# Routing of the second layer's tokens placed between the last steps of the attention before it

## The chip, the core and the metric

The kernel runs on one core of a Trainium2 chip. The metric is the device time in microseconds (us) of one execution, measured from outside the core; smaller is better. The engines are PE (TensorE, matrix products and transposes), ACT (ScalarE), DVE (VectorE), POOL (GpSimd) and SP (SyncE, which here only issues DMA transfers). Each has its own stream of instructions and takes them in order; they wait for one another by semaphores.

## What is computed

The reference is a stack of two layers over 2048 tokens of 256 values, each layer an attention on a small context and then a feed-forward part with experts:

```python
x = x + tanh(g_xattn[0]) * L0_xattn(layernorm(x), ctx)
x = x + tanh(g_ffn[0])   * L0_ffn(layernorm(x))
x = x + tanh(g_xattn[1]) * L1_xattn(layernorm(x), ctx)
x = x + tanh(g_ffn[1])   * L1_ffn(layernorm(x))
```

`L1_ffn` takes the softmax of 16 router logits `x @ router_w.T` for each token, keeps the four best experts, and adds to their weighted outputs a shared network that is scaled by a sigmoid of one more logit. So the second routing needs, for every token, the mean and deviation of the x that the second attention has just updated.

## The kernel before, in words

The 2048 tokens are 16 tiles of 128, `NT = 16`, held in `x_sb`; a pair is two neighbouring tiles (pair 7 is tiles 14 and 15).

**The second attention** (`attn1_pe`, `attn1_act`, `attn1_dve`, `attn1_pool`, `attn1_sp`) goes over `NQ = 128` steps, 8 per tile, each with two of the 16 heads. In a step PE makes two banks of logits (L1291), DVE takes their minima (L1397), ACT the exponentials (L1364), SP issues one DMA transpose of them (L1534), and four steps later PE multiplies the transposed counts with the values (`weighted`, L1303, eight small products). Once a tile's eight steps are through, DVE normalises it (`normalised`, L1403 and L1405). Once a pair's two tiles are normalised, its **output chain** runs: four transposes on PE (`output_transposes`, L1312), a high half on ACT (`output_high`, L1370), the low half on DVE (`output_low`, L1412), two projections on PE (`project`, six products each of L269 and one for the bias, L275), the addition to x on DVE (`update`, L1418), and then mean and variance of the two tiles (`stats`, L252 and L255). The chains of the first seven pairs lie among the steps of later tiles. That of pair 7 has nothing left to lie among: the loops run 16 steps more, to `STEPS = NQ + 2 * PAIRS`, for it alone. At the end DVE adds epsilon to all 16 variances (`stats_end`, L259), and the engines meet at a barrier (`meet`).

**The second routing** starts there. POOL raises 16 columns to the power -0.5 (`inverse_deviation(4)`, L1797), DVE makes 16 biases from them (L437), and then `route_pe`, `route_act` and `route_dve` go over the eight pairs in order. A pair takes these steps, by which names the prediction calls them:

- *even*, ACT L421, and *odd*, DVE L440: the two tiles of the pair normalised into `xnf`;
- *turn*, PE L377: four transposes of 128x128 f32 into a bank of PSUM;
- *high*, ACT L425, and *low*, DVE L448: the transposed pair as two f16 halves in `xnT`;
- *logits*, PE L269 with `sb_rw`: twelve products of 17 columns;
- *scores*, DVE L452: the logits copied to `lg`.

SP writes each normalised pair to the token table in DRAM (`table_dma`, L634). After the last scores, PE begins the shared network's gate and up products (L269 with `sb_sgu`) and DVE the choice of the best experts (L462 and on). The first layer's routing runs through the same three functions.

Storage ties the routing to the attention. `xnf` holds the steps' counts and their transposes (tiles 0 to 7), and two sets of transposed queries (tiles 12 to 15). `xnT`, seen as f32 under the name `xn32`, holds the queries on their way, the normalised outputs `o_n` and the halves `o_hl` of the output chain.

## Time and profile before

| | |
|---|---|
| median of 3 runs | 922.58 us (921.42 to 922.62) |
| profiled execution, time | 927.97 us |
| profiled execution, span from first to last instruction | 926.2 us |
| PE busy | 730.8 us, 79% of the span |
| DVE busy | 689.0 us, 74% |
| POOL busy | 491.3 us, 53% |
| ACT busy | 440.2 us, 48% |
| mean granted clock of PE | 0.868 of full speed |

The profile comes from one execution, whose time is 5.39 us above the median. All start times are counted from its first instruction. A share of busy time says little here, since the stages are limited by different things; what the change touches lies between about 570 us (the last two tiles of the attention) and 631 us (the last scores). A chain of waits is a list, in order of time, of what the end of the program really hung on. A line can be that of a helper: L269 is every three-part product, so it is told apart by its operands.

### The profile page before, as it was taken

The numbers are of one execution on the slowest core, as the hardware profiler recorded it, in microseconds if no ns is written. First come the engines' busy times: TensorE is split into PE (matmuls) and PEld (weight loads), VectorE is DVE, ScalarE is ACT, GpSimd is POOL, SyncE is SP. The second block draws the span as 40 slices with busy tenths as digits, with TensorE's granted clock in tenths as the row PEclk, the third lists the DMA queues.
The fourth block names the chain that finished last, engine by engine and source line by source line (L and its number), as shares of the span: only waits on it lengthen the run. The fifth ranks groups of instructions, "written<-read, shape, count | busy, mean of one in ns | idle before, by whom it ended". The sixth has DMA issues, their size and how long they took to land.

```text
span 926.2 us, 18401 instructions
## 1 busy us (share of the span) xinstructions
PE 730.8 (79%) x5700; PEld 490.1 (53%) x5701; DVE 689.0 (74%) x1819; ACT 440.2 (48%) x1037; POOL 491.3 (53%) x607
## 2 busy tenths in 40 slices
PE   3469857678899799578787777658879999999992
PEld 1258745356665455234444444335657777775561
DVE  3968956756675866889989899838857777776774
ACT  3355324323332223588889899825133344442230
POOL 5285795556662756665444467010064444467772
PEclk9678975879999999688878897758979999999997
DMA  8024444823452221499999999921034444444334
GB/s 296 2 78 140 140 156 158 240 69 115 146 159 96 86 63 41 91 186 169 195 186 191 178 184 183 179 73 41 0 97 141 123 134 140 140 146 149 95 97 131
DMA packets 203258, 121.17 MB, mean 131 GB/s; under 512 B 146476, under 2 KB 194480, under 8 KB 203184
## 3 DMA queue, kind: packets, MB, share of 16 engines
q1 hardware_dynamic: 192816, 91.10, 40.5%
q0 software_dynamic: 10368, 29.14, 11.4%
q8 instruction: 38, 0.62, 0.3%
q14 instruction: 36, 0.29, 0.1%
HBM read 64.16 MB, written 32.98 MB: 105 GB/s over the span
## 4 chain that ended last, share of the span: by engine, by line
PE 28%; ACT 10%; DVE 8%; POOL 8%; issue 7%; DMA 4%; DVEq 2%; POOLq 1%; ACTq 0%; SPq 0%
PE PS L269 13%; POOL sb_region L720 7%; ACT sb_xnf L1364 4%; PE PS L815 4%; ACT sb_wkh L1364 3%; DVE sb_wk L1397 3%; PE PS L754 2%; DMA sb_xnf<-sb_xnf 2%; PE PS L778 2%; PE PS L1291 2%; PE PS L807 2%; PE PS L404 1%; DMA sb_wkh<-sb_wkh 1%; DVE sb_x_sb L905 1%; POOL sb_xnf L670 1%
## 5 line engine op out<-in xcount | busy, mean ns | idle before, releaser
L670 POOL DMA_INDIRECT sb_xnf<-token_table,sb_ids x120 | 115.8, 965 | 150.1 <-DVE sb_wk L970 64.8
L1397 DVE TENSOR_SCALAR_CACHE_REDUCE sb_wk<-PS 128x512 f16<-128x512 f32 x256 | 161.8, 684 | 8.2 <-PE PS L1291 6.2
L269 PE MATMUL PS<-sb_xnT,sb_sgu 128*128 128x512 f16 x528 | 126.8, 393 | 1.1 <-DVE sb_lg L452 0.6
L269 PE MATMUL PS<-sb_region,sb_wkh 128*128 x720 | 121.6, 320 | 5.3 <-issue 2.8
L838 ACT ACTIVATE sb_wk<-PS 128x512 f32<-128x512 f32 (+1 forms) x48 | 28.6, 596 | 141.6 <-PE PS L269 129.0
L269 PEld LDWEIGHTS PS<-sb_region,sb_wkh 128*128 128x128 f16 x720 | 69.3, 100 | 47.2 <-issue 14.3
L754 PE MATMUL PS<-sb_sdn,sb_wkh 128*128 128x256 f16 x544 | 72.4, 287 | 27.6 <-DVE sb_wkh L941 25.8
L1364 ACT ACTIVATE sb_wkh<-PS,sb_slotv 128x512 int16<-128x512 f32 x128 | 87.3, 705 | 12.2 <-DVE sb_wk L1397 9.5
L1364 ACT ACTIVATE sb_xnf<-PS,sb_slotv 128x512 int16<-128x512 f32 x128 | 86.9, 701 | 11.1 <-DVE sb_wk L1397 8.2
L269 PEld LDWEIGHTS PS<-sb_xnT,sb_sgu 128*128 128x128 f16 x528 | 52.5, 101 | 59.2 <-issue 8.4
L970 DVE SCALAR_TENSOR_TENSOR sb_wk<-PS,sb_sm,sb_wk 128x176 f32<-128x176 f32 x120 | 42.6, 396 | 53.5 <-ACT sb_wk L866 53.3
L754 PEld LDWEIGHTS PS<-sb_sdn,sb_wkh 128*128 128x128 f16 x544 | 54.9, 103 | 47.9 <-DVE sb_wkh L941 30.5
L815 PE MATMUL PS<-sb_region,sb_wkh 128*128 x600 | 76.3, 273 | 2.7 <-DVE sb_wa L983 2.2
L857 ACT ACTIVATE sb_wkh<-PS 128x512 f16<-128x512 f32 x60 | 35.8, 596 | 83.8 <-PE PS L778 83.8
L720 POOL DMA_INDIRECT sb_region<-slot_table,sb_place x64 | 65.4, 1022 | 18.9 <-issue 18.6
L866 ACT ACTIVATE sb_wk<-PS 128x352 f32<-128x352 f32 x60 | 27.8, 463 | 91.2 <-PE PS L269 91.2
L1291 PE MATMUL PS<-sb_wa,sb_xnf 128*128 128x512 f16 x88 | 39.7, 451 | 30.6 <-ACT sb_wkh L1364 18.7
L815 PEld LDWEIGHTS PS<-sb_region,sb_wkh 128*128 128x128 f16 x600 | 55.3, 97 | 14.8 <-issue 5.6
L933 DVE SCALAR_TENSOR_TENSOR sb_wk<-PS,sb_wk 128x512 f32<-128x512 f32 (+1 forms) x48 | 33.2, 692 | 39.9 <-ACT sb_wk L838 36.3
L1507 POOL TENSOR_TENSOR sb_region<-sb_stg,sb_region 128x704 f16<-128x704 f32 (+1 forms) x32 | 42.9, 1340 | 21.6 <-issue 18.5
L954 DVE TENSOR_TENSOR sb_wkh<-PS,sb_wkh 128x512 f16<-128x512 f32 x60 | 41.2, 687 | 17.1 <-ACT sb_wkh L857 16.5
L778 PE MATMUL PS<-sb_idf,sb_xnf 128*128 128x128 f32 x240 | 38.4, 284 | 17.6 <-DMA sb_xnf<-token_table,sb_ids 17.4
(290 smaller groups left out, 1638.6 us busy)
## 6 DMA issues: line engine op xcount, KB each, us to landing
slot_table<-sb_wa SPq DMA_DIRECT2D x60, 256.0 KB, 2.3
slot_table<-token_table SPq DMA_DIRECT2D x16, 640.0 KB
sb_stg<-gu SPq DMA_DIRECT2D x24, 352.0 KB, 4.2
sb_stg<-dn SPq DMA_DIRECT2D x24, 256.0 KB, 3.8
token_table<-sb_xnf SPq DMA_DIRECT2D x16, 256.0 KB, 4.9
sb_stg<-sgu SPq DMA_DIRECT2D x8, 352.0 KB, 5.4
sb_x_sb<-x SPq DMA_DIRECT2D x1, 2048.0 KB, 12.2
out<-sb_x_sb SPq DMA_DIRECT2D x16, 128.0 KB, 2.9
```

The costliest lines, as they stand in the source:

```text
L269: last = nc.tensor.matmul(out_, lhs(i, c), rhs(j, c), start=(c == 0 and n == 0 and not begun), stop=(c == C - 1 and n == 2 and not more))
L670: nc.gpsimd.indirect_dma_start(xg[l][:, 2 * (g % XR) + n, :], None, xw[l][:, :], bass.IndirectOffsetOnAxis(ap=ids[:, 2 * g + n:2 * g + n + ...
L720: nc.gpsimd.indirect_dma_start(y_pair[m][:, t % 2, :], None, ys[1][:, :], bass.IndirectOffsetOnAxis(ap=place[:, k, t:t + 1], axis=0))\
L754: last = nc.tensor.matmul(PS[:, first + i // 2, i % 2 * D:(i % 2 + 1) * D], wkh[:, HR * h + v, i * P:(i + 1) * P], sdn[:, j, k, :], start= ...
L778: last = nc.tensor.transpose(PS[:, 4 + s % 2, (2 * n + c) * P:(2 * n + c + 1) * P], xg[l][:, 2 * (s % XR) + n, c * P:(c + 1) * P], idf[:, :])
L815: last = nc.tensor.matmul(PS[:, 7, n * D:(n + 1) * D], wkh[0:r, 4 + 2 * u + i, (2 * c + n) * P:(2 * c + n + 1) * P], DN[l][0:r, bass.ds(e[ ...
L954: nc.vector.tensor_tensor(wkh[:, 2 * (s % 2) + 1, :], PS[:, 4 + s % 2, :], wkh[:, 2 * (s % 2), :], ALU.subtract).then_inc(e_xl[l].sem, 1)
L970: last = nc.vector.scalar_tensor_tensor(wk1[:, 2 + u, n * EI:(n + 1) * EI], PS[:, 2 * u + n, EI:EG], wv[u][:, n:n + 1], wk1[:, u, n * EI:( ...
L1291: nc.tensor.matmul(PS[:, (2 * s + h) % LB, :], q_iT[t % 3][:, pair, :], keys, start=True, stop=True).then_inc(h_qk, 1)
L1364: nc.scalar.activation(h_count[s % 4][:, h * CTX:(h + 1) * CTX], PS[:, (2 * s + h) % LB, :], ACT.Exp, scale=-1.0, bias=h_nb[u][:, h:h + 1] ...
L1397: nc.vector.tensor_scalar(h_any[(2 * s + h) % 6], PS[:, (2 * s + h) % LB, :], LEVELS, None, ALU.add, ALU.min, accum_out=h_nb[s % 3][:, h:h ...
L1507: nc.gpsimd.tensor_tensor(lo, w, hi, ALU.subtract).then_inc(stg_split[n % 4], 1)
```

## The change: what it does

The routing functions are cut into pieces (`route_turn`, `route_logits`, `route_even`, `route_high`, `route_scale`, `route_odd`, `route_low`, `route_scores`). For the first layer they are called in the same order as before. For the second layer, the calls are written out by hand behind the last attention step, among the steps of pair 7's output chain, and the barrier and the 16 extra steps of the loops are gone. The pairs come in the order 4, 5, 6, 0, 1, 2, 3, 7; in `route_turn` and the others `k` counts the places in that order, and the prediction's *turn(k)*, *low(k)* and so on go by it, so (7) is pair 7. Pairs 4, 5 and 6 are turned before the attention's last counts have left tiles 0 to 7 of `xnf`. The inverse deviations come in three pieces: 12 columns at step 113 of the attention on POOL, 2 columns behind its last step, and 2 behind the statistics of pair 7. To free `xnT`, `o_hl` gets a buffer of its own and the second `o_n` moves to `wk1`.

```diff
+        o_hl = sb("o_hl", [P, 2, 2 * D], F16)
...
+        PAIR_ORDER = (tuple(range(NT // 2)), (4, 5, 6, 0, 1, 2, 3, 7))
+        NM_ENDS = ((NT,), (NT - 4, NT - 2, NT))
+        NM_STEP = HEADS * (NT // 2 - 1) - 1
+
+        def scale_of(l, j):
+
+            return next(i + 1 for i, end in enumerate(NM_ENDS[l]) if 2 * j < end)
...
+        def route_turn(pe, l, k):
+            j = PAIR_ORDER[l][k]
+            at_least(pe, r_xn[l], 0, k + 1)
+            at_least(pe, r_xd[l], 0, k + 1)
+            at_least(pe, r_xl[l], 0, k - 1)
+            for c in range(C):
+                for i in range(2):
+                    last = nc.tensor.transpose(PS[:, k % 2, c * TB + i * P:c * TB + (i + 1) * P],
+                                               xnf[:, 2 * j + i, c * P:(c + 1) * P], idf[:, :])
+            last.then_inc(r_xT[l].sem, 1)
+
+        def route_logits(pe, l, k):
+            n = E[l] + 1
+            at_least(pe, r_xl[l], 0, k + 1)
+            at_least(pe, r_lgc[l], 0, k - 1)
+            for i in range(2):
+                t = 2 * PAIR_ORDER[l][k] + i
+                last = mm3(PS[:, 2 + k % 2, i * n:(i + 1) * n], lambda i, c: xnT[:, i, c, t * P:(t + 1) * P],
+                           lambda j, c: rw[l][:, j, c, :])
+            last.then_inc(r_lg[l].sem, 1)
...
+        def route_even(act, l, k):
+            t = 2 * PAIR_ORDER[l][k]
+            at_least(act, r_nm[l], 0, scale_of(l, t // 2))
+            nc.scalar.activation(xnf[:, t, :], x_sb[:, t, :], ACT.Identity, bias=nmr[:, t:t + 1],
+                                 scale=rstd[:, t:t + 1]).then_inc(r_xn[l].sem, 1)
...
-            act.wait_ge(rstd_ready, 2 + 3 * l)
-            at_least(act, r_nm[l], 0, 1)
...
+        def route_scale(dve, l, ready, first, end):
+            dve.wait_ge(rstd_ready, ready)
+            nc.vector.scalar_tensor_tensor(nmr[:, first:end], mv[:, first:end, 0], -1.0, rstd[:, first:end], ALU.mult, ALU.mult)\
+                .then_inc(r_nm[l].sem, 1)
...
-            for j in range(NT // 2):
-                at_least(sp, r_xn[l], 0, j + 1)
-                at_least(sp, r_xd[l], 0, j + 1)
+            for k, j in enumerate(PAIR_ORDER[l]):
+                at_least(sp, r_xn[l], 0, k + 1)
+                at_least(sp, r_xd[l], 0, k + 1)
...
-        o_n = [xn32[:, u * D:(u + 2) * D] for u in (2, 14)]
-        o_hl = xn32[:, 6 * D:8 * D].bitcast(F16).rearrange("p (h n) -> p h n", h=2)
+        o_n = [xn32[:, 2 * D:4 * D], wk1[:, 3, :]]
...
-            meet(pe, 3)
+            for k in range(BEHIND):
+                weighted(NQ - BEHIND + k)
+                if k < 3:
+                    route_turn(pe, 1, k)
+                if 1 <= k:
+                    route_logits(pe, 1, k - 1)
+            last_ = GROUPS - 1
+            output_transposes(last_)
+            route_turn(pe, 1, 3)
+            route_turn(pe, 1, 4)
+            project(last_, 0)
+            project(last_, 1)
+            route_logits(pe, 1, 3)
+            for k in range(5, NT // 2):
+                route_turn(pe, 1, k)
+                route_logits(pe, 1, k - 1)
+            route_logits(pe, 1, NT // 2 - 1)
...
-            meet(act, 3)
+            route_even(act, 1, 0)
+            route_even(act, 1, 1)
+            route_high(act, 1, 0)
+            route_even(act, 1, 2)
+            route_high(act, 1, 1)
+            at_least(act, h_pv, 0, NQ)
+            route_even(act, 1, 3)
+            route_high(act, 1, 2)
+            route_even(act, 1, 4)
+            output_high(GROUPS - 1)
+            route_high(act, 1, 3)
+            route_even(act, 1, 5)
+            route_high(act, 1, 4)
+            route_even(act, 1, 6)
+            route_high(act, 1, 5)
+            route_high(act, 1, 6)
+            route_even(act, 1, 7)
+            route_high(act, 1, 7)
...
+                if s == NM_STEP:
+                    stats_end(0, NM_ENDS[1][0])
+                if s == NM_STEP + 7:
+                    route_scale(dve, 1, 5, 0, NM_ENDS[1][0])
+            stats_end(NM_ENDS[1][0], NM_ENDS[1][1])
+            route_odd(dve, 1, 0)
+            route_odd(dve, 1, 1)
+            route_scale(dve, 1, 6, NM_ENDS[1][0], NM_ENDS[1][1])
+            route_low(dve, 1, 0)
+            route_odd(dve, 1, 2)
+            route_low(dve, 1, 1)
+            route_scores(dve, 1, 0)
+            normalised(NT - 1)
+            route_odd(dve, 1, 3)
+            route_low(dve, 1, 2)
+            route_scores(dve, 1, 1)
+            route_odd(dve, 1, 4)
+            output_low(GROUPS - 1)
+            route_low(dve, 1, 3)
+            route_odd(dve, 1, 5)
+            route_scores(dve, 1, 2)
+            route_low(dve, 1, 4)
+            route_odd(dve, 1, 6)
+            update(GROUPS - 1)
+            stats(NT - 2, NT - 1)
+            stats_end(NM_ENDS[1][1], NT)
+            route_scores(dve, 1, 3)
+            route_low(dve, 1, 5)
+            route_scores(dve, 1, 4)
+            route_low(dve, 1, 6)
+            route_scores(dve, 1, 5)
+            route_scale(dve, 1, 7, NM_ENDS[1][1], NT)
+            route_odd(dve, 1, 7)
+            route_scores(dve, 1, 6)
+            route_low(dve, 1, 7)
+            route_scores(dve, 1, 7)
...
+                if s == NM_STEP + 2:
+                    inverse_deviation(4, 0, NM_ENDS[1][0])
...
-            inverse_deviation(4)
+            inverse_deviation(5, NM_ENDS[1][0], NM_ENDS[1][1])
+            inverse_deviation(6, NM_ENDS[1][1], NT)
...
-            route_act(act, 1)
...
-            route_dve(dve, 1)
...
-            route_pe(pe, 1)
```

On PE, from the product of step 124 (L1303 before, L1337 after: `weighted`) to the shared network's first products (with `sb_sgu`). Before:

```order
L1303 MATMUL PS<-sb_Vi,sb_wkh 128x16 x16
L1303 MATMUL PS<-sb_Vi,sb_xnf 128x16 x16
L1312 MATMUL PS<-sb_idf,sb_xnT 128x128 x4
L269 MATMUL PS<-sb_wqp,sb_xnT 128x256 x6
L275 MATMUL PS<-sb_brow,sb_ones_h 128x256
L269 MATMUL PS<-sb_wqp,sb_xnT 128x256 x6
L275 MATMUL PS<-sb_brow,sb_ones_h 128x256
L377 MATMUL PS<-sb_idf,sb_xnf 128x128 x8
L269 MATMUL PS<-sb_rw,sb_xnT 128x17 x12
L377 MATMUL PS<-sb_idf,sb_xnf 128x128 x4
```

After, from behind the same product of step 124 (turns are L383, logits L270 with `sb_rw`, output transposes L1346):

```order
L383 MATMUL PS<-sb_idf,sb_xnf 128x128 x4
L1337 MATMUL PS<-sb_Vi,sb_wkh 128x16 x8
L383 MATMUL PS<-sb_idf,sb_xnf 128x128 x4
L270 MATMUL PS<-sb_rw,sb_xnT 128x17 x12
L1337 MATMUL PS<-sb_Vi,sb_xnf 128x16 x8
L383 MATMUL PS<-sb_idf,sb_xnf 128x128 x4
L270 MATMUL PS<-sb_rw,sb_xnT 128x17 x12
L1337 MATMUL PS<-sb_Vi,sb_xnf 128x16 x8
L270 MATMUL PS<-sb_rw,sb_xnT 128x17 x12
L1346 MATMUL PS<-sb_idf,sb_wk 128x128 x4
L383 MATMUL PS<-sb_idf,sb_xnf 128x128 x8
L270 MATMUL PS<-sb_wqp,sb_o_hl 128x256 x6
```

The products of steps 125 to 127 now stand behind turns and logits, and the output transposes behind the logits of three pairs; two more turns stand ahead of the projections.

On DVE, the end of the new order, from the update of pair 7 (L1484) to the choice of experts (L497); nmr is the bias column, lg the scores, and L463, L469, L476 are odd, low and scores:

```order
L1484 SCALAR_TENSOR_TENSOR sb_x_sb<-PS,sb_tgw,sb_x_sb 128x512
L253 BN_STATS sb_bst<-sb_x_sb 128x6 x2
L256 BN_AGGR sb_mv<-sb_bst 128x2 x2
L260 TENSOR_SCALAR sb_ve<-sb_mv 128x2
L476 TENSOR_SCALAR sb_lg<-PS 128x34
L469 TENSOR_TENSOR sb_xnT<-PS,sb_xnT 128x2x256
L476 TENSOR_SCALAR sb_lg<-PS 128x34
L469 TENSOR_TENSOR sb_xnT<-PS,sb_xnT 128x2x256
L476 TENSOR_SCALAR sb_lg<-PS 128x34
L458 SCALAR_TENSOR_TENSOR sb_nmr<-sb_mv,sb_rstd 128x2
L463 TENSOR_SCALAR sb_xnf<-sb_x_sb,sb_mv,sb_rstd 128x256
```

Behind the update only three scores and two lows stand between the epsilon (L260) and the bias of the last two tiles (L458); before, all eight pairs followed.

## Rows read from the trace of the kernel before

**Rows 1.** Chain of waits around the attention's last output chain: start us, us, what

```profile
601.29 3.09 DMA sb_xnf<-sb_xnf
...
604.43 0.40 PE PS L1303 x8
...
605.66 1.13 PE PS L1312 x4
...
606.81 0.61 ACT sb_xnT L1370
...
608.18 1.46 PE PS L269 x6
...
611.39 0.75 DVE sb_x_sb L1418
...
613.64 2.92 POOL sb_rstd L1797
```

**Rows 2.** Chain of waits through the second routing, same columns

```profile
616.95 0.61 ACT sb_xnf L421
617.65 1.10 PE PS L377 x4
618.77 0.61 ACT sb_xnT L425
619.40 0.70 DVE sb_xnT L448
620.15 0.49 PE PS L269 x12
...
630.21 0.51 PE PS L269 x12
```

**Rows 3.** Timeline of ACT: start, us, engine, line, operation [idle before <-releaser]

```profile
600.90 0.21 ACT L1364 ACTIVATION_READ_ACCUMULATOR sb_xnf<-PS,sb_slotv 128x1 f32 x1
...
616.95 1.09 ACT L421 ACTIVATE sb_xnf<-sb_x_sb,sb_nmr,sb_rstd 128x256 f32<-128x256 f32 x2 [9.54 <-DVE sb_nmr L437]
```

**Rows 4.** Timeline of DVE from the last maxima to the choice of experts

```profile
600.99 0.25 DVE L255 BATCH_NORM_AGGREGATE sb_mv<-sb_bst 128x2 f32<-128x6 f32 x2
...
616.75 0.73 DVE L440 TENSOR_SCALAR sb_xnf<-sb_x_sb,sb_mv,sb_rstd 128x256 f32<-128x256 f32 x2
...
622.27 0.69 DVE L448 TENSOR_TENSOR sb_xnT<-PS,sb_xnT 128x512 f16<-128x512 f32 x1 [0.78 <-ACT sb_xnT L425]
622.88 0.18 DVE L452 TENSOR_SCALAR sb_lg<-PS 128x34 f32<-128x34 f32 x1
622.98 0.40 DVE L440 TENSOR_SCALAR sb_xnf<-sb_x_sb,sb_mv,sb_rstd 128x256 f32<-128x256 f32 x1
...
630.74 0.19 DVE L452 TENSOR_SCALAR sb_lg<-PS 128x34 f32<-128x34 f32 x1 [0.49 <-PE PS L269]
```

**Rows 5.** Timeline of PE, same columns

```profile
601.86 0.38 PE L1303 MATMUL PS<-sb_Vi,sb_wkh 128*128 128x16 f16 x8 [1.03 <-DMA sb_wkh<-sb_wkh]
...
620.52 1.09 PE L377 MATMUL PS<-sb_idf,sb_xnf 128*128 128x128 f32 x4
621.40 0.52 PE L269 MATMUL PS<-sb_rw,sb_xnT 128*128 128x17 f16 x12
...
630.99 5.39 PE L269 MATMUL PS<-sb_xnT,sb_sgu 128*128 128x512 f16 x17 [0.29 <-DVE sb_lg L452]
```

**Rows 6.** POOL: groups by form (count, busy us, mean ns), and its timeline

```profile
L1797 POOL TENSOR_TENSOR sb_rstd<-sb_ve,sb_mhalf 128x12 f32<-128x12 f32 x1 | 2.3, 2307 | 6.5 <-DVE sb_ve L259 6.5
...
613.64 2.91 POOL L1797 TENSOR_TENSOR sb_rstd<-sb_ve,sb_mhalf 128x16 f32<-128x16 f32 x1 [30.39 <-DVE sb_ve L259]
```

**Rows 7.** Stretches: busy (count) of PE, PEld, DVE, ACT, POOL, then granted clock, DMA share

```profile
622.00:627.00 5.00, 4.68 (x51) 3.70 (x51) 3.84 (x10) 3.98 (x8) 0.00 (x0) 0.50 0.48 169
...
631.00:636.00 5.00, 5.00 (x17) 1.96 (x17) 4.76 (x51) 0.65 (x2) 0.00 (x0) 0.68 0.00 0
```

**Rows 8.** The page's DMA issues: KB each, median us to landing

```profile
token_table<-sb_xnf SPq DMA_DIRECT2D x16, 256.0 KB, 4.9
```

More of the change, by code:

```diff
@@ L413, in tiles_pe, with route_high @@
                              skip_group_check=True).then_inc(r_texp[l].sem, 1)
-        def route_act(act, l):
-            act.wait_ge(rstd_ready, 2 + 3 * l)
-            at_least(act, r_nm[l], 0, 1)
-            for j in range(NT // 2 + 1):
-                if j < NT // 2:
-                    t = 2 * j
-                    nc.scalar.activation(xnf[:, t, :], x_sb[:, t, :], ACT.Identity, bias=nmr[:, t:t + 1],
-                                         scale=rstd[:, t:t + 1]).then_inc(r_xn[l].sem, 1)
-                if j >= 1:
-                    at_least(act, r_xT[l], 0, j)
-                    nc.scalar.activation(xnT[:, 0, :, (j - 1) * TB:j * TB],
-                                         PS[:, (j - 1) % 2, :].rearrange("p (c n) -> p c n", c=C), ACT.Copy).then_inc(r_xh[l].sem, 1)
+        def route_even(act, l, k):
[3 more added lines that the diff above has]
+                                 scale=rstd[:, t:t + 1]).then_inc(r_xn[l].sem, 1)
+        def route_high(act, l, k):
+            j = PAIR_ORDER[l][k]
+            at_least(act, r_xT[l], 0, k + 1)
+            nc.scalar.activation(xnT[:, 0, :, j * TB:(j + 1) * TB],
+                                 PS[:, k % 2, :].rearrange("p (c n) -> p c n", c=C), ACT.Copy).then_inc(r_xh[l].sem, 1)
+        def route_act(act, l):
+            act.wait_ge(rstd_ready, 2)
+            for k in range(NT // 2 + 1):
+                if k < NT // 2:
+                    route_even(act, l, k)
+                if k >= 1:
+                    route_high(act, l, k - 1)
         def softmax_act(act, l):
@@ L456, in best_dve @@
+        def route_dve(dve, l):
+            route_scale(dve, l, 2, 0, NT)
+            route_odd(dve, l, 0)
+            for k in range(NT // 2 + 1):
+                if k + 1 < NT // 2:
+                    route_odd(dve, l, k + 1)
+                if k < NT // 2:
+                    route_low(dve, l, k)
+                if k >= 1:
+                    route_scores(dve, l, k - 1)
         def best_dve(dve, l):
@@ L1328, in attn1_pe @@
             at_least(pe, s_accr[0], 0, BLK)
-            for s in range(STEPS):
+            for s in range(NQ):
                 if s + AHEAD < NQ:
                     logits(s + AHEAD)
-                if BEHIND <= s < NQ + BEHIND:
+                if s >= BEHIND:
                     weighted(s - BEHIND)
@@ L1373, in attn1_act @@
             at_least(act, s_d[0], 0, NSH)
-            for s in range(STEPS):
+            for s in range(NQ):
                 t, pair = s // PAIRS, s % PAIRS
-                if s < NQ:
-                    exponentials(s)
+                exponentials(s)
                 if s == 1:
@@ L1418, in update @@
                 nc.vector.scalar_tensor_tensor(xt, o_bank, tgw[:, 1:2], xt, ALU.mult, ALU.add).then_inc(o_x, 1)
-            for s in range(STEPS):
+            for s in range(NQ):
                 t, pair = s // PAIRS, s % PAIRS
-                if s < NQ:
-                    maxima(s)
+                maxima(s)
                 if s < 2:
@@ L1454, in attn1_dve @@
                     stats(2 * o, 2 * o + 1)
-            stats_end(0, NT)
-            meet(dve, 3)
+                if s == NM_STEP:
[34 more added lines that the diff above has]
+            route_scores(dve, 1, 7)
         items = []
```

60 lines of the change are left out of this document (21 added, 39 removed).

## The prediction

> **What bounds the kernel now.** I read the chain of waits first, around the last attention step. The last transposed counts are issued at 601.29 and land for the product of step 127 at 604.43. Then comes a relay with one engine at work at a time: output transposes 605.66, high half 606.81, projections 608.18, update 611.39, statistics and epsilon, the power on POOL 613.64, the first even 616.95 [rows 1, 2]. The reader should see that each piece hands over to another engine, so that nearly every microsecond is latency. Then the second routing: even 616.95, turn 617.65, high 618.77, low 619.40, logits 620.15, eight pairs through the same ring, last logits 630.21, last scores 630.74 [rows 2, 4]. DVE's choice of experts and PE's shared products follow at once, the latter at 630.99 [rows 5]. From there DVE is busy 4.76 of 5 us [rows 7]. So the stretch from 601.29 to 630.74 lies bare on the path, and what follows should move with the last scores. The timelines of ACT, DVE and PE give the paces, the group of POOL the price of a power. The stretches give PE's clock: 0.50 of full speed through the routing [rows 7].
>
> **Step prices.** From start to start, in us, each from two rows. Even: 0.70 until PE can turn (616.95 to 617.65), about 0.5 until ACT takes the next (two last 1.09, one 0.61) [rows 2, 3]. Turn: 1.12 until ACT (617.65 to 618.77), 0.88 of PE (620.52 to 621.40) [rows 2, 5]. High: 0.63 until DVE (618.77 to 619.40), about 0.5 of ACT, taken as even's. Low: 0.75 until PE (619.40 to 620.15), 0.61 of DVE (622.27 to 622.88) [rows 2, 4]. Scores: 0.10 of DVE (622.88 to 622.98); odd: about 0.36 (two last 0.73) and, with the hand-over to PE, 0.45 until a turn [rows 4]. Logits: 0.53 until the scores (630.21 to 630.74) [rows 2, 4]; of PE I take 0.36, an estimate from their row of 0.52, whose last part overlaps what follows [rows 5]. The product of a step: 0.42 until DVE, 0.25 of PE, estimated the same way from 0.38 [rows 5]; normalising 0.81 until PE, so that product and normalising make the 1.23 from 604.43 to 605.66 [rows 1]. Output transposes 1.15 until ACT; high and low 1.37 together; the two projections 3.21 until the update (608.18 to 611.39), 1.47 of PE for the first; update, statistics and epsilon 2.25 until POOL (611.39 to 613.64), 2.0 of it on DVE [rows 1]. A check: the old loop, reckoned with these prices from 616.95, has its last scores at 630.60; they came at 630.74.
>
> **What the change costs and brings.** The removed parts are two. The 16-column power, the wait for it and the whole routing no longer follow the update; and two rounds of hand-over disappear with the barrier. Nothing is saved in work: all eight pairs are still turned. It is laid between the waits, in strict order on each engine, so I walk it through.
>
> *The start.* ACT's last exponential ends at 601.11 (600.90 + 0.21) [rows 3], and even(0), even(1) follow at 601.00 (the accumulator's read overlaps) and 601.50. DVE ends statistics of tiles 12 and 13 at 601.24 [rows 4], epsilon for two columns at 601.31, odd(0) at 601.40. Turn(0) starts at 601.85. POOL starts the two-column power at 601.57. Its price is not in the trace: 12 columns took 2.31, 16 took 2.92 [rows 1, 6], so a straight line gives some 0.8 for two, the top is 2.92. I take 1.2, nearer the low end, since the slope between the two rows is clear, with 0.4 for a fixed part. Then the bias comes at 602.8, ahead of low(0) at 603.60, and costs nothing. If the power took 2.9, low(0) and all behind it on DVE would wait.
>
> *The four last products.* They keep their inputs: step 125's came at 601.86, step 127's at 604.43 [rows 1, 5]. But on PE they now stand behind turns and logits: turn(0) 601.85, product 125 at 602.73, turn(1) 602.98, logits(0) 604.35 (waiting for low(0)), product 126, turn(2) 604.96, logits(1) 605.84, product 127 at 606.20. That is 1.8 later than before. DVE normalises at 606.62. Meanwhile high(2) waits on ACT behind the order that even(3) needs product 127: high(2) 607.12, low(2) 607.75, logits(2) 608.50, and only behind them the output transposes, at 608.86, 3.2 later than before. This is the price of the interleaving.
>
> *The output chain.* Turn(3) and turn(4) take PE until 611.52, which is when the projections start; the high and low halves (610.01 and 610.64, done at 611.38) are hidden behind them. Projections until 614.46, update at 614.70, 3.3 later than before. In those waits DVE and ACT have done the evens and odds up to (6) and the lows up to (4).
>
> *After the update.* DVE: statistics and epsilon until 616.78, then scores(3), low(5) 616.88, scores(4), low(6) 617.81, scores(5), bias 618.52. PE: logits(3), turn(5) 614.82, logits(4), turn(6) 616.06, logits(5) 617.63. POOL's last power starts at 616.95 and ends at 618.2, just inside DVE's own queue, so it costs nothing; at 2.9 it would end at 619.9. Then pair 7 alone: even 618.81, turn 619.51, high 620.63, low 621.26, logits 622.01, last scores 622.54.
>
> So update to last scores takes 7.8 instead of 19.3 (611.39 to 630.74), 11.5 gained, and 3.3 of that is given back by the later update. Sum: 630.74 - 622.54 = 8.2; the check above was 0.1 short, so I take **8.1**.
>
> *Beside other work.* The 12-column power at step 113 and its bias: POOL idles 30.39 before the old power [rows 6], so 2.3 plus its wait only push the last weight splits into that gap; if the gap were gone they would delay the shared weights, needed only at 622. DVE's share in the steps is two instructions of about 0.2, under 0.4 if none of it falls in a wait; against 8.1 I leave it in the range. SP's eight stores to the token table start at about 602 instead of 617; SP has the last transposes issued by then (601.29). They are needed at the row lists, 20 us after the last scores, and the last one now starts 1 us after even(7) as before. The new buffers move no work.
>
> Against the profiled execution the sum gives 927.97 - 8.1 = 919.9. That execution stands 5.4 above the median; nothing in the moved stretch explains those, so against the median it is 922.58 - 8.1 = **914.5**.
>
> **Rivals.**
> *PE's clock rises in the tail.* It was 0.50 in 622 to 627 although PE was busy 4.68 of 5; in 631 to 636, products without a break from 630.99, it averaged 0.68, so it went from 1.2 to 2.4 GHz after about 3.2 us [rows 7, 5]. In the walk PE has no gap from 608.86 to 616.9. If the clock rises at 613, PE's steps halve, but DVE's queue after the update holds: last scores 621.8, gain 8.9, 913.7; at the earliest, 612.5, they are at 621.05, 913.0. For it: the stretch is twice as long as 3.2. Against: five of its eight microseconds are turns and logits, during which the clock stayed down before.
> The Trainium skill's page "TensorE: Matmul & The Clock Gate" (section "Part 1: The HAM clock gate") says that the low rate is the default and that sustained activity releases it. By that rule this rival would come true; the stretch from 631 agrees, that from 622 does not.
>
> *The small powers cost as much as the large.* Two-column powers of 2.9 each: the bias at 604.6 holds low(0) by 1.0, and the second power adds 1.5 behind the scores. Walked through: last scores 625.05, gain 5.6, **917.1**. For it: 12 and 16 columns differ by only 0.6 [rows 1, 6]. Against: that is more than in proportion.
>
> *The stores collide with the last transposes (slower).* Three pairs' stores are issued before product 127, a store's median to landing is 4.9 [rows 8]. If the transposes of steps 125 to 127 each had to wait out one store, they would be 4.9, 9.8 and 14.7 late, and the walk ends at 635.5: 4.8 slower than before, **927.4**. It decides from 10 us of delay at product 127 on; less still leaves a gain, as PE comes to it 1.8 late anyway. Against: the transposes are issued first, on the same queue, and the stores moved at a DMA share of 0.48 [rows 7], far from full.
>
> *The gain is swallowed behind.* Some wait of the expert stage (stores, shared weights, first gathers) takes the 8 us back: 922.6. DVE's 4.76 of 5 [rows 7] speaks against.
>
> *The clock stays high from the start of the tail.* Everything on PE halves from 601.9 on: last scores 618.9, gain 11.7, 910.9. Nothing in the trace holds it up there.
>
> **Chances.** The walk 0.50, the clock's rise 0.22, the dear powers 0.15, clock high throughout 0.04, swallowed 0.06, collision 0.03. The range takes in the first three: from 913.0 less the spread of the runs shown (1.2) to 917.1 plus 1.2, **911.8 to 918.3**. A measurement can tell 0.2%, here 1.85 us, from no change. Faster by more: 0.50 + 0.22 + 0.15 + 0.04 = 0.91; within it 0.06; slower 0.03.
>
> **What would show it.** In the new profile: product 127 about 606.2 and update near 614.7, both later than before; the last scores near 622.5, with the steps behind unchanged in length; the two-column powers at 1.0 to 1.4; the last four products not waiting for DMA; a granted clock of 0.50 from 602 to 622. The forecast is wrong if the last scores keep their place, if a power of two columns takes 2 or more, or if the expert stage has a new wait.

## The result, and the profile after

| | before | changed |
|---|---|---|
| median | 922.60 us (921.42 to 925.54, 4 runs) | 913.02 us (912.74 to 915.69, 4 runs) |
| ratio | | 0.9892, 95% interval 0.9870 to 0.9915 |
| profiled execution: time, span | 927.97, 926.2 us | 915.69, 913.9 us |

The changed kernel is faster by 9.6 us, where 8.1 was forecast. The two profiled executions differ by 12.3, and 2.85 of this lies ahead of the change: the aggregate of tiles 12 and 13, the last thing both kernels do alike, starts at 600.99 before [rows 4] and at 598.14 now. The executions of one kernel spread by more than that ahead of this mark (e8 below), so I don't count it as the change's. I measure the **tail**, from the start of this aggregate to the start of the last scores, and subtract 2.85 from each time of the prediction's walk (its step-by-step times) before I compare. Before, the tail is 29.75 us.

The page of the changed kernel: the header, part 1, and the counts that say that no work went.

```profile
span 913.9 us, 18405 instructions
PE 729.3 (80%) x5700; PEld 490.9 (54%) x5701; DVE 692.0 (76%) x1823; ACT 440.6 (48%) x1037; POOL 494.2 (54%) x609
```

PE and DVE are as busy as ever. The time went out of the waits, and the chain of waits shows where (start us, us, what), against [rows 1, 2]:

```profile
599.10 1.10 PE PS L383 x4
...
602.09 0.21 PE PS L1337 x8
602.30 0.95 PE PS L383 x4
603.25 0.31 PE PS L270 x12
603.56 0.23 PE PS L1337 x8
...
606.16 0.95 PE PS L1346 x4
607.11 1.71 PE PS L383 x8
608.82 1.28 PE PS L270 x6
...
611.53 0.75 DVE sb_x_sb L1484
...
615.28 0.61 ACT sb_xnf L433
615.93 0.67 PE PS L383 x4
616.62 0.61 ACT sb_xnT L439
617.25 0.70 DVE sb_xnT L469
...
618.00 0.50 PE PS L270 x12
...
618.53 0.19 DVE sb_lg L476
```

In this stretch no DMA and no POOL stands in the chain any more. The first turn is where the chain had waited for a DMA transposition, product 127 (603.56, L1337) follows straight behind other work of PE, and behind the update there is one pair's ring, from 615.28 to 618.53, where there were eight. The timelines give the pieces that the prediction had timed. PE, with its longest wait ahead of the projections (for low(2)):

```profile
599.98 0.41 PE L1337 MATMUL PS<-sb_Vi,sb_wkh 128*128 128x16 f16 x8
603.41 0.36 PE L1337 MATMUL PS<-sb_Vi,sb_xnf 128*128 128x16 f16 x8
605.67 0.49 PE L270 MATMUL PS<-sb_rw,sb_xnT 128*128 128x17 f16 x12 [1.90 <-DVE sb_xnT L469]
606.01 1.09 PE L1346 MATMUL PS<-sb_idf,sb_wk 128*128 128x128 f32 x4
```

POOL, both small powers; and DVE from the aggregate to the last scores:

```profile
598.72 0.81 POOL L1898 TENSOR_TENSOR sb_rstd<-sb_ve,sb_mhalf 128x2 f32<-128x2 f32 x1 [15.53 <-DVE sb_ve L260]
613.77 0.70 POOL L1898 TENSOR_TENSOR sb_rstd<-sb_ve,sb_mhalf 128x2 f32<-128x2 f32 x1 [14.24 <-DVE sb_ve L260]
```

```profile
598.14 0.25 DVE L256 BATCH_NORM_AGGREGATE sb_mv<-sb_bst 128x2 f32<-128x6 f32 x2
...
599.56 0.16 DVE L458 SCALAR_TENSOR_TENSOR sb_nmr<-sb_mv,sb_rstd 128x2 f32<-128x2 f32 x1 [0.28 <-POOL sb_rstd L1898]
...
611.53 0.75 DVE L1484 SCALAR_TENSOR_TENSOR sb_x_sb<-PS,sb_tgw,sb_x_sb 128x512 f32<-128x512 f32 x1 [0.87 <-PE PS L276]
...
614.99 0.18 DVE L476 TENSOR_SCALAR sb_lg<-PS 128x34 f32<-128x34 f32 x1
615.09 0.15 DVE L458 SCALAR_TENSOR_TENSOR sb_nmr<-sb_mv,sb_rstd 128x2 f32<-128x2 f32 x1
...
618.53 0.19 DVE L476 TENSOR_SCALAR sb_lg<-PS 128x34 f32<-128x34 f32 x1 [0.58 <-PE PS L270]
```

The power was finished at 614.47, and the bias (L458) was taken at 615.09 without an idle time before it: DVE's own queue held it, as predicted. Last, stretches of the tail: busy us (count) of PE, PEld, DVE, ACT, POOL, then granted clock, DMA share, GB/s.

```profile
606.00:611.00 5.00, 5.00 (x31) 4.21 (x28) 2.76 (x7) 2.65 (x5) 0.00 (x0) 0.50 0.35 121
611.00:613.00 2.00, 2.00 (x36) 1.76 (x34) 1.38 (x3) 0.60 (x1) 0.00 (x0) 0.99 0.55 197
613.00:615.00 2.00, 0.51 (x13) 0.37 (x12) 1.85 (x9) 0.60 (x1) 0.70 (x1) 1.00 0.01 4
615.00:617.00 2.00, 0.94 (x16) 0.83 (x16) 0.66 (x5) 0.97 (x2) 0.00 (x0) 1.00 0.09 33
617.00:619.00 2.00, 0.71 (x13) 0.53 (x14) 1.18 (x6) 1.50 (x2) 0.00 (x0) 0.72 0.32 107
```

The clock went up at about 611.0, from 1.2 to 2.4 GHz, after five microseconds in which PE was never idle, and stayed up until after 617. So the prediction's first rival came true here, and not its base case of 0.50. The tail is 20.39 us, 9.36 shorter. From the last scores to the end of the span it is 295.4 us (913.9 - 618.53) against 295.5 before (926.2 - 630.74), so these two profiles show nothing given back. Second profiles of the same two kernels have 297.2 (e1) and 295.1 (e8), so this part alone is known to some 2 us only.

### The profile page after: what moved, and what is told of

Read it like the earlier page. It is cut to its first block, busy times and chain, and to the rows that moved or that the text cites. A ratio compares the mean times of both kernels' runs of the same rounds, so it can differ in the third digit from the quotient of the medians.

```text
span 913.9 us, 18405 instructions
## 1 busy us (share of the span) xinstructions
PE 729.3 (80%) x5700; PEld 490.9 (54%) x5701; DVE 692.0 (76%) x1823; ACT 440.6 (48%) x1037; POOL 494.2 (54%) x609
## 4 chain that ended last, share of the span: by engine, by line
PE 28%; DVE 9%; ACT 8%; POOL 8%; issue 7%; DMA 4%; DVEq 2%; POOLq 1%; ACTq 0%
PE PS L270 14%; POOL sb_region L755 7%; PE PS L850 4%; ACT sb_xnf L1414 4%; DVE sb_wk L1463 3%; ACT sb_wkh L1414 3%; PE PS L789 2%; DMA sb_xnf<-sb_xnf 2%; PE PS L813 2%; PE PS L1325 2%; DMA sb_wkh<-sb_wkh 2%; PE PS L842 2%; PE PS L419 1%; DVE sb_x_sb L940 1%; POOL sb_xnf L705 1%
## 5 line engine op out<-in xcount | busy, mean ns | idle before, releaser
L270 PE MATMUL PS<-sb_xnT,sb_sgu 128*128 128x512 f16 x528 | 128.1, 395 | 1.1 <-DVE sb_lg L476 0.6
L270 PE MATMUL PS<-sb_region,sb_wkh 128*128 x720 | 121.3, 320 | 5.1 <-issue 2.6
L270 PEld LDWEIGHTS PS<-sb_region,sb_wkh 128*128 128x128 f16 x720 | 69.2, 99 | 46.0 <-issue 13.1
L270 PEld LDWEIGHTS PS<-sb_xnT,sb_sgu 128*128 128x128 f16 x528 | 52.7, 101 | 59.8 <-issue 9.5
L989 DVE TENSOR_TENSOR sb_wkh<-PS,sb_wkh 128x512 f16<-128x512 f32 x60 | 41.2, 687 | 16.3 <-ACT sb_wkh L892 15.8
## 6 DMA issues: line engine op xcount, KB each, us to landing
sb_x_sb<-x SPq DMA_DIRECT2D x1, 2048.0 KB, 12.2
```

Of the source, the lines that this page charges most:

```text
L270: last = nc.tensor.matmul(out_, lhs(i, c), rhs(j, c), start=(c == 0 and n == 0 and not begun), stop=(c == C - 1 and n == 2 and not more))
L989: nc.vector.tensor_tensor(wkh[:, 2 * (s % 2) + 1, :], PS[:, 4 + s % 2, :], wkh[:, 2 * (s % 2), :], ALU.subtract).then_inc(e_xl[l].sem, 1)
```

## The experiments

**The theory** is the walk of the prediction, refined by the trace: the gain is latency taken out of two relays, about a third of it from cutting the power and the rest from laying routing into the waits, and some 3 us are lost again because the hand-written order lets PE wait for low(2) ahead of the output transposes. **Rivals**: most of the gain comes from the higher clock; the small powers matter more (or less) than thought; the stores, which now start earlier, hold up the last transposes.

All tails, from the aggregate of tiles 12 and 13 to the last scores, each from one profile; *product 127* and *update* are counted from the aggregate:

| kernel | aggregate at | product 127 | update | tail |
|---|---|---|---|---|
| before | 600.99 | 3.44 | 10.40 | 29.75 |
| e8 before, again | 591.95 | 3.53 | 10.49 | 29.84 |
| changed | 598.14 | 5.27 | 13.39 | 20.39 |
| e1 changed, again | 595.93 | 5.27 | 13.18 | 20.18 |
| e6 changed, stores held | 593.68 | 5.27 | 13.48 | 20.48 |
| e2 pieces only | 595.99 | 3.45 | 10.47 | 26.52 |
| e3 dear powers | 599.39 | 6.91 | 14.08 | 23.81 |
| e4 reordered | 597.50 | 5.12 | 11.32 | 17.75 |
| e5 reordered, stores held | 595.99 | 5.15 | 11.37 | 17.79 |
| e7 reordered, clock kept | 597.62 | 5.20 | 10.88 | 17.76 |
| e9 reordered, DVE +24 | 597.70 | 5.05 | 11.25 | 17.68 |
| e10 reordered, ACT +24 | 595.04 | 3.40 | 9.61 | 16.04 |
| e11 as e5, again | 596.36 | 5.00 | 11.21 | 17.63 |

**e8** is the kernel before, once more.

> The kernel before once more, for its profile alone. In its first profile the aggregate of tiles 12 and 13 starts at 600.99, in the four profiles of changed kernels at 595.9 to 599.4. If that is the spread of executions, this one starts between 596 and 601 and the stretch from there to the last scores is 29.7 us again. If the change also speeds up the steps before, it is at 600 or above.

918.64 us (span 916.9), one execution. Its tail is 29.84, within 0.1 of the other profile's, but it starts at 591.95, below the 596 to 601 that were expected, where the other one started at 600.99. So the way to the tail differs by up to 9 us between executions of one kernel, and the tail doesn't: a comparison of whole times says little about a change of 2 us, one of tails says it well. **e1** is the changed kernel once more.

> The changed kernel again, on the chip of the next three runs, so that they can be compared with it and not only with the kernel before. Both theories: 0.989 of the kernel before, within 0.9870 to 0.9915. On the clock: if its rise at the end of the projections belongs to the order of the work, it stands again between the first projection and the update, and last statistics of step 127 to last scores takes 20.1 us within 0.8; if it was luck, the clock stays at 0.50 and the stretch takes 21.3.

915.60 us, ratio 0.9899 (0.9871 to 0.9926). Tail 20.18, again with the clock's rise.

**e2** keeps the power in three pieces and the new buffers, but puts the routing behind the statistics again, in the new order of pairs:

```diff
-            for k in range(BEHIND):
-                weighted(NQ - BEHIND + k)
-                if k < 3:
-                    route_turn(pe, 1, k)
-                if 1 <= k:
-                    route_logits(pe, 1, k - 1)
+            weighted(NQ - BEHIND + 0)
...
+            weighted(NQ - BEHIND + 3)
             output_transposes(last_)
...
+            route_turn(pe, 1, 0)
...
```

> All routing steps stand behind pair 7's update (in the order 4, 5, 6, 0, 1, 2, 3, 7); the inverse deviations stay in three pieces and the barrier stays away. Theory of the walk: product 127 and the projections come back to their old places (no delay of 3.3 us), the power and its wait (3.3 us from 613.38 to the first even) leave the path, and the whole routing loop follows: 3.3 us faster than the kernel before, 5 to 6.5 slower than the changed kernel. Rival, that most of the gain is the power in pieces and the barrier's going: at least 7 us faster than before, within 2.5 of the changed kernel.

920.53 us, ratio 0.995 (0.992 to 0.998). The tail is 26.52, 3.23 shorter than before, where 3.3 was expected; and product 127 and the update keep their distance from the aggregate. So of the 9.36 of the change, 3.2 belong to the pieces, the barrier and the new order of pairs together, and 6.1 to the interleaving, net of what it gives back; the rise of the clock, which e2 doesn't have (0.50 from 599 to 623), is part of these 6.1. By medians e2 is only 4.9 slower than e1, just under the 5 to 6.5 that were expected; whole times spread too much to decide between 4.9 and 6.1.

**e3** puts a 16-column power of spare numbers, which nobody reads, ahead of each two-column power.

```diff
+                if n >= 5:
+                    nc.gpsimd.tensor_tensor(spare[:, n - 5, :], lower[:, 0, 0:NT], mhalf[:, :], ALU.pow)
                 nc.gpsimd.tensor_tensor(rstd[:, first:end], ve
```

> A power of 16 columns into a spare buffer ahead of each of the two-column powers (2.9 us more each; nothing of the result hangs on it). Theory of the walk: the first holds low(0) by 2.0 us, the second the last even by about 2.5; together 3.5 to 4.0 us slower than the changed kernel. Rival, that the powers are hidden well enough for their size not to matter: slower by less than 1 us.

919.22 us, ratio 0.9932 (0.9910 to 0.9954). Its timelines of POOL and of DVE:

```profile
599.96 3.02 POOL L1900 TENSOR_TENSOR sb_spare<-sb_lower,sb_mhalf 128x16 f32<-128x16 f32 x1 [15.65 <-DVE sb_ve L261]
602.95 0.70 POOL L1901 TENSOR_TENSOR sb_rstd<-sb_ve,sb_mhalf 128x2 f32<-128x2 f32 x1
```

```profile
603.68 0.16 DVE L459 SCALAR_TENSOR_TENSOR sb_nmr<-sb_mv,sb_rstd 128x2 f32<-128x2 f32 x1 [3.15 <-POOL sb_rstd L1901]
...
619.29 0.16 DVE L459 SCALAR_TENSOR_TENSOR sb_nmr<-sb_mv,sb_rstd 128x2 f32<-128x2 f32 x1 [2.19 <-POOL sb_rstd L1901]
```

The tail is 3.4 longer than the changed kernel's, a little under the 3.5 to 4.0 that were expected (3.6 by the medians of e3 and e1). About 0.5 of this isn't the power's own: from bias to last scores e3 takes 3.91 where the change takes 3.44, because the clock is at 0.50 from 618.5 on. Against the change the idle time before the bias is 3.15 instead of 0.28, and 2.19 instead of none. So the price of the power decides as the prediction's second rival said, and only where it exceeds what DVE has queued; at 0.70 to 0.81 it is free.

**e4** leaves the work as it is and changes the order alone: the output transposes, and all that they wait for, stand ahead of low(2).

```diff
-PE:  w0 turn0 w1 turn1 logits0 w2 turn2 logits1 w3 logits2 out turn3 turn4 p0 p1 logits3 turn5 logits4 ...
+PE:  w0 w1 turn0 turn1 w2 w3 turn2 logits0 out turn3 turn4 p0 p1 logits1 turn5 logits2 turn6 logits3 logits4 ...
-DVE: odd0 odd1 scale low0 odd2 low1 scores0 norm odd3 low2 scores1 odd4 outlow low3 ...
+DVE: odd0 odd1 scale odd2 low0 norm odd3 low1 odd4 low2 outlow scores0 low3 low4 ...
```

(These two pairs of lines sum up the calls, and are not the kernel's text. w0 to w3 are products 124 to 127, out the output transposes, p0 and p1 the projections. ACT's order is changed to match.)

> The same steps in another order, found by laying the same step prices out again: on PE turns (0) and (1) behind the product of step 125, product 127 directly behind 126, and the output transposes behind only one set of logits; the scores gathered behind the update. Theory of the walk: product 127 is at its old place (1.8 us earlier than in the changed kernel), the update 2.9 us earlier, last scores 3.5 us earlier: 3.5 us (3.0 to 4.0) faster than the changed kernel, 0.985 of the kernel before. Rival, that what bounds the tail is DVE's own work behind the update and not the place of the update: within 1 us of the changed kernel.

912.52 us, ratio 0.9867 (0.9840 to 0.9893). The tail is 2.6 shorter than the changed kernel's, where 3.5 was expected. The chain has the missing part:

```profile
597.80 4.77 DMA sb_xnf<-sb_xnf
...
602.62 0.38 PE PS L1337 x8
```

The transposed counts of step 127 took 4.77 us from issue to landing, where they had taken 3.09 before [rows 1]. In the changed kernel this is covered, since product 127 comes late anyway. I took it for the collision that the prediction's third rival had named, at a third of its price, and tried it.

**e5** and **e6** hold back every store to the token table until ACT, DVE and PE have done with step 127's product; e5 in the order of e4, e6 in the change's.

```diff
+            if l == 1:
+                at_least(sp, h_pv, 0, NQ)
             for k, j in enumerate(PAIR_ORDER[l]):
```

> The reordered kernel with SP holding the eight stores to the token table until the product of step 127 is done. In the reordered kernel without this, the transposition of step 127 took 4.77 us from its issue instead of 3.09 and PE waited 1.8 us for it, with DMA engines full. Theory, that the stores take DMA time from the last transposes: product 127 comes 3.4 us after the start of the last two-tile aggregate (604.43 - 600.99 before), the last transposition takes 3.1 to 3.3 us, and the stretch from that aggregate to the last scores is 17.0 us or a little less instead of 17.75, with the update 1 to 1.7 us earlier. Rival, that the late transposition was chance or comes from what ACT and PE do: it takes 4.8 again and nothing moves.

> The changed kernel with the same hold on SP. There product 127 stands behind 1.8 us of routing on PE, so a transposition that is 1.7 us late is just hidden. Theory: no difference from the changed kernel, stretch from the aggregate of tiles 12 and 13 to the last scores 20.2 to 20.4 us; the stores' later end is needed by nobody. Rival, that the stores cost the changed kernel as well: 1 us or more shorter.

e5: 908.86 us, ratio 0.9852 (0.9832 to 0.9871); e6: 913.10 us, ratio 0.9904 (0.9885 to 0.9924). In e5 the transposition is as late as ever, with no store anywhere near it:

```profile
596.34 4.76 DMA sb_xnf<-sb_xnf
...
601.14 0.38 PE PS L1339 x8
```

The tail is 17.79, that of e4. So it isn't the stores that make the transposition late, and my explanation fell. e6's tail is 20.48, that of the changed kernel to 0.1. That e5's median is 3.7 below e4's is no merit of the wait: the tails are equal, and e11, the same kernel in another job, had 912.05.

**e7** is meant to hold PE's clock up: three products of 512 columns, which nobody reads, are added to each of the steps 120 to 127 and to two of the last four products, in the order of e5.

```diff
+            def warm():
+                for n in range(3):
+                    nc.tensor.matmul(PS[:, 7, :], idh[:, :], wqp[:, 0, 0, :], start=True, stop=True)
...
+                if s >= NQ - 8:
+                    warm()
```

> The kernel with the reordering and the hold, and in addition three products of 512 columns that nobody reads behind each of the steps 120 to 127 of the loop and behind two of the last products, so that PE's clock is not let down. Theory: the granted clock stays at 1.0 from the last steps to the projections, turns take 0.44 us of PE instead of 0.88, projections 0.8 instead of 1.5, and the stretch from the aggregate to the last scores is 15.5 to 16.5 us. Rival, that DVE and ACT set the tail and PE's rate does not matter there, or that the products cost what they bring: 17 us as without them.

910.82 us, ratio 0.9868 (0.9848 to 0.9887). Two of its stretches, columns as above:

```profile
596.00:599.00 3.00, 2.69 (x35) 1.42 (x34) 2.52 (x11) 2.72 (x8) 0.80 (x1) 1.00 1.02 191
602.00:605.00 3.00, 1.79 (x28) 1.45 (x28) 1.71 (x5) 1.79 (x4) 0.00 (x0) 1.00 0.29 98
```

The tail is 17.76, against 17.79 in e5, where the clock was 0.50 for the first ten microseconds. But e7 didn't hold the clock to the end, as a later stretch and the same part of e5 show:

```profile
612.40:615.40 3.00, 2.01 (x28) 1.43 (x28) 1.68 (x5) 2.24 (x3) 0.00 (x0) 0.50 0.28 93
```

```profile
611.00:612.60 1.60, 1.04 (x20) 0.72 (x17) 1.10 (x4) 1.32 (x4) 0.00 (x0) 1.00 0.36 124
```

And pair 7's turn, in the chain of e7 and in that of e5:

```profile
612.34 1.11 PE PS L383 x4
```

```profile
611.19 0.66 PE PS L383 x4
```

Counted from the aggregate, e7 is 0.48 ahead of e5 at the update and still at the bias (13.87 against 14.35). It loses 0.45 of it in pair 7's ring, which takes 3.89 from bias to last scores at the low rate, and 3.44 in e5 at the high one. So the equal tails are two effects of the clock that cancel: 0.5 ahead of the update and 0.45 behind it. The rival "it is all the clock" is not borne out for the reordered kernels, since each effect is small against the 12 us by which e5's tail is shorter than that of the kernel before. But PE's rate does matter there, and with the clock up to the end the tail should be 0.45 shorter (an estimate from these two rings; no run shows it). For the change's own order it wasn't tried; there the trace gives the clock's share (below).

**e9, e10, e11** go after the late transposition. In the records of completions, 15 of its 16 parts land in time (in e5 by 599.53) and one at 601.10; before, all 16 land together. In each of the seven profiles so far with routing mixed in, a packet of 16 KB of instructions starts 0.42 to 0.50 us ahead of the 15th part; in the three others it starts over a microsecond behind the landing. So I tried to move that packet, on the guess that DVE's or ACT's stream fetches it: 24 instructions more, which write a tile that nobody reads, on DVE (e9) or ACT (e10), some hundreds of microseconds ahead of the tail. e11 is e5 again.

```diff
+            for i in range(24):
+                nc.vector.memset(spare[:, i:i + 1], 0.0)
             nc.vector.memset(kT_odd[0:P // 2], 0.0)
```

```diff
             act.wait_ge(p_sv, 1)
+            for i in range(24):
+                nc.scalar.activation(spare[:, i:i + 1], svw[:, 0:1], ACT.Copy)
```

> The reordered kernel with held stores, with 24 tiny memsets more on VectorE (into a tile that nobody reads) long before the tail, where the keys are laid apart, so that everything VectorE does in the tail is 24 instructions further on in its stream. Theory (the last piece of step 127's transposition lies behind a 16 KB fetch of instructions, and the fetch is VectorE's): the fetch, which fell about 3.2 us after the aggregate of tiles 12 and 13 in e5, comes earlier by what VectorE needs for 24 instructions there (2 us or more), ahead of the transposition's last part; that transposition then takes 3.2 us, not 4.8, product 127 starts 1.5 us sooner, and the tail is 16.3 us from the aggregate to the last scores, not 17.8; the kernel is at 907.5 us where e5 was at 908.9. Rival 1 (the fetch is another engine's): the fetch and the late landing stay, the tail is 17.8. Rival 2 (the fetch and the late piece have nothing to do with each other): the fetch moves and the transposition still takes 4.8 us, tail 17.8.

> The reordered kernel with held stores, with 24 tiny copies more on ScalarE (into a tile that nobody reads) long before the tail, in the preparation of the values. Theory with the fetch as ScalarE's: the fetch comes 2 us or more earlier than 3.2 us after the aggregate of tiles 12 and 13, step 127's transposition takes 3.2 us instead of 4.8, the tail is 16.3 us. Rival 1 (the fetch is VectorE's or another engine's): fetch and late landing stay, tail 17.8 us. Rival 2 (no link between the two): the fetch moves, the transposition still takes 4.8 us, tail 17.8 us.

> The reordered kernel with held stores again, unchanged, in the same job as the two with 24 instructions more, as their control: every theory expects the transposition of step 127 at 4.7 to 4.9 us, a tail of 17.8 us, and a ratio to before of 0.985 within 0.003.

913.83, 910.22 and 912.05 us; ratios 0.9910 (0.9885 to 0.9935), 0.9882 (0.9855 to 0.9909) and 0.9901 (0.9875 to 0.9928). The chain of e11, the control, and that of e10:

```profile
596.66 4.66 DMA sb_xnf<-sb_xnf
...
601.36 0.38 PE PS L1339 x8
```

```profile
595.26 3.14 DMA sb_xnf<-sb_xnf
...
598.44 0.39 PE PS L1342 x8
```

e9 is e11 over again (4.69, tail 17.68). In e10 the transposition is back at 3.14, product 127 at 3.40 behind the aggregate as in the kernel before, and the tail is 16.04, where 16.3 was expected of a landing in time. **What a late landing costs here is thereby shown: 1.6 us** (a tail of 17.63 to 17.79 in e4, e5, e9 and e11, which have it, and of 16.04 in e10, which hasn't), all of it still there at the end of the tail. What e10 did to the packet is less than I had expected. Half a microsecond of DMA traffic around it, in e11 and in e10:

```profile
GB/s 205 143 185 184 247 164 164 144 164 185 164 102 103 103 82 82 62 61 42 41 21 41 20 41 41 20 1311 0 0 0 0 0 0 0 0 0 0 0 0 0
```

```profile
GB/s 225 205 225 246 266 143 225 143 143 102 164 205 123 225 287 185 186 165 124 103 1434 143 124 102 123 102 103 41 63 41 42 21 1 0 0 0 0 0 0 0
```

These are 40 slices from 599.0 (e11) and from 597.5 (e10). The spike is the packet. In e11 it starts at 599.33, as the last of the transposition drains, and one part is missing for 1.5 us behind it. In e10 it starts at 597.76, which is 0.59 us ahead of the 15th part where e11 has 0.46, with more traffic on all sides, and nothing is late: all 16 parts land by 598.40. Both the theory "24 instructions earlier, 2 us or more" and the rival "nothing moves" are wrong: the packet lies 0.1 to 0.2 us earlier (2.50 behind the issue of the transposition, not 2.67), and the transposition is in time. In the other nine profiles with routing mixed in, it lay 0.42 to 0.50 ahead of the 15th part.

That ACT's 24 instructions moved it is unlikely. There are packets of 8 KB as well, and those did move: one that starts 14.6 us behind the aggregate in e11 (DVE's 1839th instruction in the trace) starts at 7.3 in e9 (its 1841st), and one 12.2 ahead of it in e11 (ACT's 1055th) starts 17.3 ahead in e10 (its 1059th). So these follow the streams of DVE and of ACT. The 16 KB packet doesn't: it comes at ACT's 1120th instruction in e10 and at the 1093rd to 1098th in the twelve other profiles; in e9 it comes at DVE's 1834th, and in the others at the 1804th to 1810th. The early landing of e10 is then the spread of one execution, as far as the record shows: luck.

To have more than one spot, I went through all 13 profiles: 4628 transfers whose first 15 parts land within 1 us. In 116 of them the last part is over 0.8 us behind. Of the 206 ahead of whose 15th landing (0.3 to 1.8 us) a packet of instructions starts, 106 are late; of the other 4422, 10. So a late last part nearly always has such a packet ahead of it, and in half of the cases where the packet comes at that moment, the part is late. The moment alone doesn't decide: from 0.4 to 0.5 us ahead 14 of 26 are late, from 0.5 to 0.7 only 2 of 30, from 0.7 to 1.0 again 17 of 27. That the part queues behind the packet on one DMA engine is my reading of this; no record names the engine.

## Why the prediction was right

By its steps, each less 2.85 us for the earlier start:

| step | predicted | measured |
|---|---|---|
| turn(0) | 599.00 | 599.10 |
| product 125 | 599.88 | 599.98 |
| logits(0) | 601.50 | 601.60 |
| product 127 | 603.35 | 603.41 |
| logits(2) | 605.65 | 605.67 |
| output transposes | 606.01 | 606.01 |
| projections | 608.67 | 608.61 |
| update | 611.85 | 611.53 |
| bias for tiles 14, 15 | 615.67 | 615.09 |
| even(7) | 615.96 | 615.28 |
| last scores | 619.69 | 618.53 |

**The walk** holds to 0.1 us through its first ten microseconds. Its prices came from one loop of the second routing and held among the attention's last products, too: on each engine the rows stand in the order in which the calls are written. That product 127 starts 1.8 later and the output transposes 3.2 later, *the price of the interleaving*, is right, and e4 shows that it was avoidable: 2.6 us of tail, and 4.35 in e10, where the late landing is absent.

**The clock.** The step that was mis-sized is the rate of PE behind the update. The prediction took 0.50 for the base case and gave a rise of the clock 0.22. It rose at about 611.0; the rival had said 610.2 (613 less 2.85). With it turn(7) is done in 0.69 instead of 1.12 (615.93 to 616.62), and the turns and logits that follow the projections, up to logits(5), cost DVE no wait. The rival's gain was 8.9 and its time 913.7; measured are 9.4 in the tail and 913.0 in the median. The time thus came into the range by the rival's path, at 1.2 us from its lower end; the prediction's sign of a clock of 0.50 up to 622 didn't come true. The Trainium skill's page "TensorE: Matmul & The Clock Gate" (section "Part 1: The HAM clock gate") says that the low rate is the default and sustained activity releases it. In this stretch the trace agrees: PE was busy 5.00 of 5 at 0.50, then 0.99. The prediction had held against a rise that the clock stayed down through the turns and logits of the old routing; but these left gaps (4.68 of 5 [rows 7]), and 606 to 611 has none. e2 agrees: with gaps left between its turns it stays at 0.50 throughout. That the gaps are the reason is an inference from these rows; no run puts gaps into the new stretch. In e3 the clock rises at 611.7, behind 3.1 us in which PE was busy 3.10.

**The power** was taken at 1.2 and took 0.81 and 0.70. The straight line through 12 and 16 columns gave 0.8 and came out; the 0.4 that I added for a fixed part didn't. That it came out is partly luck, for the trace of the kernel before had one more size, which the prediction missed:

```profile
L1797 POOL TENSOR_TENSOR sb_rstd<-sb_ve,sb_mhalf 128x4 f32<-128x4 f32 x1 | 1.4, 1380 | 0.0
```

Four columns took 1.38, 0.3 more than the line has, and a line through 4 and 12 columns would have given 1.15 for two. Why four columns are dearer stays open. The time does not depend on it, as the prediction said and e3 shows from the other side.

**The sum.** Predicted tail 21.55 (600.99 to 622.54), measured 20.39, 20.18 and 20.48 in three profiles. The term that was mis-sized is thus the same one, PE's rate. About 0.3 of the difference is there by the update (the end of the projections ran at the higher rate already), another 0.3 by the bias, and the rest in pair 7's ring: 3.44 from bias to last scores where 4.02 was predicted (and 3.91 and 3.89 measured in e3 and e7, where the clock was low there). So some 1.2 of the 9.4 are the clock's, and by this reckoning the rival that most of the gain is the clock's falls. With the median 922.6, less 9.4, one gets 913.2.

**The rivals that fell.** The expert stage took nothing back that these runs can show (295.4 against 295.5 us, repeats 297.2 and 295.1; the medians differ by 9.6, more than the tails do). The stores started under the last transposes and cost nothing; holding them back moved neither tail (e5 against e4, e6 against the change). The late landing, which has the look of such a collision at a third of its price (1.6 against 4.9 a store), is present with and without them. The prediction's sentence that the last products would *not* wait for DMA holds for the change, with 0.17 us to spare: the last part of step 127 landed at 603.24, and its product had its turn at 603.41.

## What to carry to other kernels

A relay of short steps between engines can be costed by walking it through in strict order on each engine, with prices from start to start of one loop; here this held to 0.1 us per step over ten microseconds, but the rate of PE has to be asked again wherever the new order closes its gaps. When work is laid into waits, put only what nobody behind it in the same queue has to wait for: the same pieces, in an order with the output transposes ahead of one low half, gave 2.6 us more (e4 moved several calls at once, so it isn't shown which of them counts). And compare stages by marks inside the trace: from one execution to the next the way to this tail differs by 9 us, while the tail itself repeats to 0.3.

The fastest kernels of the study are the reordered ones: e5 at 0.9852 (0.9832 to 0.9871), the same kernel again as e11 at 0.9901 (0.9875 to 0.9928), and e10 at 0.9882 (0.9855 to 0.9909), each against the kernel before in its own job. Their intervals overlap; by the tail e10 is the shortest, by 1.75 us against e5, in the one execution that was profiled.

## What the runs showed of the hardware

- A power on GpSimd takes 0.70 to 0.81 us for two columns and 2.90 to 3.02 for sixteen, in a straight line with the 2.31 of twelve columns [rows 6]; at (2.92 - 2.31) / 4, or 0.15 us a column, the fixed part of about 0.5 (an estimate) lies within those 0.7. Four columns took 1.38, 0.3 above that line.
- An SBUF transposition of 3.1 to 3.2 us took 4.7 to 4.9 in the profiles where a 16 KB packet of instructions starts in its last half microsecond. It did not when the packet started behind the landing (before, e2, e8), nor in the one profile where it started 0.13 us earlier (e10).
- The streams of DVE and ACT are seen in packets of 8 KB; the 16 KB packets follow neither. Who fetches these stays open, with PE the candidate: around the tail they are about 253 PE instructions apart in the trace (8508 - 6989 over six packets before), and e7, with 30 products and as many weight loads more, has 39 of them where each other kernel has 38. Against it, the packet at the transposition kept its time in e7 (3.1 behind the aggregate, as in e5), and only later ones moved.
- PE's clock rose at the end of five unbroken microseconds of transposes and products (of 3.1 in e3), and stayed at 1.00 from 611 to 617 with PE busy for less than half of the time from 613 on.
- The low rate costs pair 7's ring, from bias to last scores, about 0.45 us: 3.89 and 3.91 at 0.50 (e7, e3), 3.44 at 1.00 (the change, e5).
